# Second-block attention as one software pipeline, with probability blocks turned by 32x32 VectorE transposes and on-chip transfers

## What is computed

```python
x = x + ga * attention(h)            # h = layernorm(x) * (1 + ca) + sa
q = (h @ w_q).reshape(B, S, 8, 4, 128)       # 32 query heads in 8 groups of 4
k = (h @ w_k).reshape(B, S, 8, 128)          # one key head for each group
v = (h @ w_v).reshape(B, S, 8, 128)
scores = einsum('bqhgd,bkhd->bhgqk', q, k) * 128 ** -0.5
scores = where(causal, scores, -inf)
probs  = softmax(scores)
attn   = einsum('bhgqk,bkhd->bqhgd', probs, v).reshape(B, S, 4096)
out    = attn @ w_o
```

## Time and profile before

| | us |
|---|---|
| median of 3 runs | 2140.12 |
| lowest, highest run | 2139.69, 2142.99 |
| span of the profiled execution | 2136.5 |
| PE busy in it | 2033.7 (95%) |
| DVE busy | 1254.4 (59%) |
| ACT busy | 920.2 (43%) |
| POOL busy | 443.5 (21%) |

### The profile page before, as it was taken

One profiled execution on the slowest core, in us unless ns is written; L12 is line 12 of the kernel. 1 busy time (PEld: TensorE's weight loads), 2 busy tenths in 40 slices (PEclk: granted clock), 3 DMA queues, 4 the chain that ended last, 5 costly groups with the idle time before them and its releaser, 6 DMA issues. The chain is left out here.

```text
span 2136.5 us, 33376 instructions
## 1 busy us (share of the span) xinstructions
PE 2033.7 (95%) x10551; PEld 1705.1 (80%) x10551; DVE 1254.4 (59%) x3113; ACT 920.2 (43%) x2453; POOL 443.5 (21%) x446
## 2 busy tenths in 40 slices
PE   6589599999999999999999999999999997999999
PEld 3376388888888888888888888888888885788887
DVE  5854774746556474756756474746647475644444
ACT  3353353535435363543535363543536353623323
POOL 1601732121222122123312122121222211000000
PEclk9679699999999999999999999999999998999999
DMA  9000221000000100001200100000010005410110
GB/s 355 26 1 11 89 69 50 29 20 29 20 29 20 49 29 21 29 0 74 75 30 20 49 14 35 29 20 29 20 49 1 28 10 183 138 60 17 42 59 20
DMA packets 72186, 100.27 MB, mean 47 GB/s; under 512 B 8136, under 2 KB 32712, under 8 KB 72144
## 3 DMA queue, kind: packets, MB, share of 16 engines
q1 hardware_dynamic: 68544, 93.45, 13.0%
q10 hardware_dynamic: 3600, 6.29, 0.8%
HBM read 87.14 MB, written 12.58 MB: 47 GB/s over the span
## 5 line engine op out<-in xcount | busy, mean ns | idle before, releaser
L1121 PE MATMUL ps<-hA,wq 128*128 128x512 f32 x1536 | 384.1, 399 | 0.0
L1195 PE MATMUL ps<-wo,oT 128*128 128x512 f32 x1536 | 368.0, 394 | 0.0
L1279 ACT ACTIVATE probs<-ps,nmax 128x512 f32<-128x512 f32 (+3 forms) x512 | 268.1, 539 | 216.5 <-DVE nmax L1398 216.5
L1195 PEld LDWEIGHTS ps<-wo,oT 128*128 128x128 f32 x1536 | 282.7, 188 | 55.5
L1121 PEld LDWEIGHTS ps<-hA,wq 128*128 128x128 f32 x1536 | 280.3, 188 | 56.1
L1413 DVE TENSOR_TENSOR pt<-ps,pt 128x512 fp32r<-128x512 f32 (+2 forms) x384 | 202.2, 554 | 166.7 <-ACT pt L1289 166.7
L1178 PE MATMUL ps<-pt,V 128*128 128x512 f32 (+2 forms) x1152 | 258.6, 353 | 0.0
L1398 DVE CUSTOM_DVE_ANT_0 ps<-ps,mask 128x512 f32<-128x512 f32 (+3 forms) x512 | 234.6, 519 | 28.3 <-PE ps L1155 28.3
L1155 PE MATMUL ps<-kT,qT 128*128 128x512 f32 (+2 forms) x1152 | 232.7, 346 | 1.1 <-DVE qT L1382 1.1
L1289 ACT ACTIVATE pt<-ps 128x512 fp32r<-128x512 f32 (+2 forms) x384 | 190.5, 496 | 65.8 <-PE ps L1166 64.9
L1155 PEld LDWEIGHTS ps<-kT,qT 128*128 128x128 f32 x1152 | 195.9, 188 | 28.2 <-issue 1.5
(11 more groups left out here) (210 smaller groups left out, 2806.3 us busy)
## 6 DMA issues: line engine op xcount, KB each, us to landing
wq_in<-in_L_attn_w_q_dram SPq DMA_DIRECT2D x17, 1024.0 KB, 7.0
wo_in<-in_L_attn_w_o_dram SPq DMA_DIRECT2D x16, 1024.0 KB, 5.3
wm<-in_L_wmod_dram SPq DMA_DIRECT2D x3, 2048.0 KB, 13.2
wk_in<-in_L_attn_w_k_dram SPq DMA_DIRECT2D x17, 256.0 KB, 2.8
wv_in<-in_L_attn_w_v_dram SPq DMA_DIRECT2D x17, 256.0 KB, 3.3
X<-in_L_attn_x_dram SPq DMA_DIRECT2D x4, 1024.0 KB, 10.6
wm_a<-in_L_wmod_dram SPq DMA_DIRECT2D x2, 2048.0 KB, 22.5
x_mid<-X SPq DMA_DIRECT2D x16, 256.0 KB, 2.0
```

The costliest lines, as they stand in the source:

```text
L1121: last = nc.tensor.matmul(ps[:, bank, :], w[i][:, c, cols], hT[k][:, c, b * S:(b + 1) * S], start=(c == 0 and n == 0), stop=(c == DC - 1 a ...
L1195: last = nc.tensor.matmul(ps[:, bank, :], oT[x_][:, b, h, r * P:(r + 1) * P], wo[y_][:, h, :], start=(h == 0 and n == 0), stop=(h == GQ - ...
L1279: nc.scalar.activation(pe_[:, u % 2, PO[i]:PO[i] + KEYS[i]], ps[:, BANK_S + bank, col:col + KEYS[i]], ACT.Exp, bias=nmax[:, u % 2, i:i + 1 ...
```

## The change

Nothing of the mathematics changes, and no other stage. The changed parts:

- **No PE transposes of probabilities.** POOL, not DVE, multiplies the exponentials by the reciprocal row sum (`body` of POOL, new L1081). DVE turns each 32x32 square in place with five transposes (`turn_quadrants`, new L1454, L1456) into `tp`, which has one buffer. SP then moves the squares across partitions, 16 transfers of 32 partitions x 320 elements (40 KB) for each unit, from `tp` to `pd` (new L992), which has two buffers. ACT makes the high part in one copy of 1280 columns (`p_high`, new L1324), DVE the low part in one subtraction (`p_low`, new L1462). `outputs` reads and writes the four quadrants by a pattern with steps (new L1164).
- **One pipeline.** `scores(u)` runs two units ahead of `outputs(u - 2)`, across the border of two groups. W2 to W7 of a group run in the first five units of the next; K and V of the next group in the last three units of this one. Each pair has an own first body, a loop over the six middle groups, an own last body, and a `flush`.
- **Other moves.** The exponentials have one buffer, not two. The weight loads move from SP's queue to ACT's, ahead of `o_high` in unit 0. Q has one bank, K and V share one, W has two. The gate transposes move from the front to the `flush` of each pair, and so do the load, the normalising and the turning of the next pair's rows. The renamed semaphores (`chosen`, `chain`, `consts`) stand for the same waits.

The diff, cut to its core (the old `turn`, `scale_rows` and `t_part` go):

```diff
+            QD = 32
+            NQD = P // QD
+            SLOTS = 10
+            BW = SLOTS * QD
+            PVS = [(0, 0, 4 * QD), (1, 4 * QD, 7 * QD), (2, 8 * QD, 10 * QD)]
...
-                pe_ = sb(at, "probs", [P, 2, PW], F32)
+                pe_ = sb(at, "probs", [P, PW], F32)
+                tp = sb(at, "tp", [P, NQD, BW], F32)
+                pd = sb(at, "pd", [P, 2, NQD, BW], F32)
+                pt = [sb(at, f"pt{i}", [P, NQD, BW], F32R) for i in range(2)]
...
+                def landed_of(g, u):
+
+                    return landed[u % 2], 256 * (UNITS // 2 * g + (u // 2 + 1))
...
+                            for u in range(UNITS):
+
+                                sp.wait_ge(t_done, UNITS * g + (u + 1))
+                                for a_ in range(NQD):
+                                    for b_ in range(NQD):
+                                        sp.dma_start(pd[QD * b_:QD * (b_ + 1), u % 2, a_, :],
+                                                     tp[QD * a_:QD * (a_ + 1), b_, :]).then_inc(landed[u % 2], 16)
...
+                                pool.wait_ge(rinv_done, UNITS * g + (u + 1))
+                                nc.gpsimd.sem_inc(waits_seen, 1)
+                                for i in range(TB - 1, -1, -1):
+                                    v = pe_[:, PO[i]:PO[i] + KEYS[i]]
+                                    nc.gpsimd.tensor_scalar(v, v, rinv[:, u % 2, i:i + 1], None, ALU.mult).then_inc(scaled, 1)
...
+                        def body(g, first, last):
+                            for u in range(UNITS):
+                                scores(g, u)
+                                if u >= 2 or not first:
+                                    outputs(g, u - 2)
+                                if u == 0:
+                                    turn_v(g, 0)
+                                if u == 4:
+                                    turn_v(g, 1)
+                                if u < 6:
+                                    q_project(g, u + 2)
+                                elif not last:
+                                    q_project(g + 1, u - 6)
+                                if u < 4 and not first:
+                                    out_project(g - 1, u + 2)
+                                if u == 4 and not first:
+                                    out_project(g - 1, 6)
+                                    out_project(g - 1, 7)
+                                if u >= 6:
+                                    out_project(g, u - 6)
+                                if u == 1:
+                                    k_project(g, 1)
+                                if u == 3:
+                                    v_project(g, 1)
+                                if u == 5 and not last:
+                                    k_project(g + 1, 0)
+                                if u == 7 and not last:
+                                    v_project(g + 1, 0)
...
+                        def p_high(g, u):
+                            act.wait_ge(*landed_of(g, u))
+                            reached(act, o_full, UNITS * g + u)
...
+                        def turn_quadrants(g, u):
+
+                            reached(dve, *landed_of(g, u - 1))
+                            to = tp[:].rearrange("p b (s j) -> p s b j", j=QD)
+                            for n, t in enumerate(range(TB - 1, -1, -1)):
+                                dve.wait_ge(scaled, UNITS * TB * g + (TB * u + n + 1))
+                                whole = min(t + 1, TB - 1)
+                                p = pe_[:, PO[t]:PO[t] + KEYS[t]].rearrange("p (s b j) -> p s b j", b=NQD, j=QD)
+                                last = nc.vector.transpose(out=to[:, t:t + 3 * whole - 2:3], in_=p[:, 0:whole])
+                                if t == TB - 1:
+                                    nc.vector.transpose(out=to[:, 7:8], in_=p[:, TB - 1:TB])
+                            last.then_inc(t_done, 1)
```

More of the change, by code:

```diff
@@ new lines, in project, with q_project @@
+                        def project(bank, w, cols, b, done):
+                            for c in range(DC):
+                                for n, (i, k) in enumerate(((0, 0), (0, 1), (1, 0))):
+                                    last = nc.tensor.matmul(ps[:, bank, :], w[i][:, c, cols], hT[k][:, c, b * S:(b + 1) * S],
+                                                            start=(c == 0 and n == 0), stop=(c == DC - 1 and n == 2))
+                            last.then_inc(done, 1)
+                        def q_project(g, u):
+                            h = u % GQ
+                            pe.wait_ge(wq_split, GQ * g + (h + 1))
+                            reached(pe, q_ready, UNITS * g + u)
+                            project(BANK_Q, wq, slice(h * HD, (h + 1) * HD), u // GQ, q_full)
@@ new lines, in outputs @@
+                        def outputs(g, u):
+                            slot, b = u % 2, u % UNITS // GQ
+                            reached(pe, o_ready, UNITS * g + (u + 1))
+                            if u % GQ == 0:
+                                pe.wait_ge(vt_ready, PAIR * g + (b + 1))
+                            pe.wait_ge(plo_done, UNITS * g + (u + 1))
+                            blocks = lambda v: v.rearrange("p a (t j) -> p a t j", j=QD)
+                            by_quadrant = lambda v: v.rearrange("p (t a j) -> p a t j", a=NQD, j=QD)
+                            for n, (kt, first, end) in enumerate(PVS):
+                                for k, (x_, y_) in enumerate(((0, 0), (1, 0), (0, 1))):
+                                    last = nc.tensor.matmul(by_quadrant(ps[:, BANK_O, kt * P:]), V[x_][:, b, kt, :],
+                                                            blocks(pt[y_][:, :, first:end]),
+                                                            start=(n == 0 and k == 0), stop=(n == 2 and k == 2))
+                                if n == 1:
+                                    nc.tensor.matmul(by_quadrant(ps[:, BANK_O, 3 * P:]), v_last[:, b, :],
+                                                     blocks(pd[:, slot, :, LAST]), start=False, stop=False)
+                            last.then_inc(o_full, 1)
@@ new lines, in prologue, with body @@
+                        def prologue(pair, g):
+                            k_high(g, 0)
+                            q_high(g, 0)
+                            v_copy(g, 0)
+                            q_high(g, 1)
+                        def body(g, first, last):
+                            more = not (last and g == NG - 1)
+                            for u in range(UNITS):
+                                if u == 0 and not first:
+                                    v_copy(g, 0)
+                                if u == 2:
+                                    k_high(g, 1)
+                                if u == 4:
+                                    v_copy(g, 1)
+                                if u == 6 and not last:
+                                    k_high(g + 1, 0)
+                                exps(g, u)
+                                if u == 0:
+                                    load_out(g)
+                                    if more:
+                                        load_next(g)
+                                if u >= 2 or not first:
+                                    o_high(g, u - 2)
+                                if u in (0, 4):
+                                    v_high(g, u // 4)
+                                if u >= 1 or not first:
+                                    p_high(g, u - 1)
+                                if u < 6:
+                                    q_high(g, u + 2)
+                                elif not last:
+                                    q_high(g + 1, u - 6)
@@ new lines, in flush @@
+                            if more:
+                                normal(1)
+                            o_low(g, -1)
+                            if more:
+                                parts(0)
+                            add_out(g - 1, 4)
+                            add_out(g - 1, 5)
+                            if more:
+                                parts(1)
+                            add_out(g - 1, 6)
+                            add_out(g - 1, 7)
+                        over_pairs(dve, prologue, body, flush)
```

835 lines of the change are left out of this document (401 added, 434 removed).

## The result

The changed kernel takes **2458.6 us** (median of 4 runs, 2456.75 to 2462.51), the kernel before in the same session 2140.57 (2139.69 to 2142.99). The ratio is 1.149, with a 95% interval of 1.1474 to 1.1506: 318 us slower. The profiled execution has a span of 2457.4 us against 2136.5, which is 320.9 more. The forecast was 2050 us with a range to 2165; the result is on the side of rival 2 and 236 us above the time that rival gave.

A forecast was written before the change was run, and what follows sets the result against it. PE, 95% busy, was taken to bound the kernel. Less work -134, pair ends +46, weight issues +8, between pairs -7, front -2: -89 on 2136.5, plus 3.6 to median: 2051, forecast 2050 us, range 2020 to 2165.

The forecast's parts named there:

- rival 2: SP's chain of sixteen issues and a landing on the one buffer `tp` sets the time: L 12.0, 2223 us; chance 0.19.
- Issues: SP's sixteen transfers of a unit, 0.39 us apart, 5.9 us to the last; bounds 0.33 and 0.50, 5.0 to 7.5 us.
- L: Shortest unit through the transfer loop of `tp`: transposes, issues, landing, hand-overs, 10.0 us against PE's 10.7; bounds 8.0 to 13.3.
- The sign that the text gave for being wrong: DVE waiting for a landing in every unit and PE for `plo_done`, through issues over 0.44 us or transposes over 2.6.
- Transposes: DVE's five instructions over 1280 columns before the transfers of a unit: 1.9 us, bounds 1.3 and 3.2.
- landing: Arrival of a unit's last 40 KB transfer after its issue: 2.0 us, bounds 1.5 and 2.4.
- the ends of the pairs: Rival 1's formula, 46 + 63 L a pair: 20 us to first transposes, 26 after the last; 92 for two.
- Weight loads beside the transfers: ACT's four weight issues delay its `o_high` and high part in unit 0 of each group: 0.5 us a group, +8 us.
- POOL's products: POOL's four scalings by the reciprocal row sum: 1.8 us a unit, 3.3 at worst, hidden under 10.7.
- PE's side: Ten transposes a unit removed, 134 us less work; a group holds 85.9 us; `outputs` runs of 32 elements cost nothing.
- The border between the pairs: PE's 11.5 us gap between the pairs shrinks as loads and normalising move beside W2 to W7: -7 us.
- rival 1: Transfer loop is the bound but a fair one, L from 10.7 to 11.3: 2097 us at 11.0; chance 0.21.

The follow-up runs named there:

- e1: Changed kernel with four of the sixteen transfers of each unit cut in halves, twenty issues for the same bytes: 2770.36 us.
- e2: Changed kernel with four transfers of the same bytes instead of sixteen, leaving out the crossing between bands of partitions (result not the reference's): 2050.41 us.
- e9: Changed kernel with eight of a unit's sixteen transfers issued by SP and eight by ACT, and the products on DVE: 2313.42 us, ratio 1.0795.
- e4: Changed kernel with weight loads cut to one row block of 16 partitions from the second group on, all issues and waits kept: 2398.67 us.
- e3: Changed kernel with the four products by the reciprocal row sum on DVE instead of POOL: 2457.82 us.
- e6: Changed kernel with the squares moved through DRAM, one write and four reads, five issues instead of sixteen: 2102.58 us, ratio 0.981.
- e7: e6 with the products by the reciprocal row sum on DVE instead of POOL: 2078.56 us, ratio 0.970.
- e5: Changed kernel with a second buffer for `tp`, so transposes wait for the landing of two units before: 2275.11 us, ratio 1.0621.
- e10: e5 with the products by the reciprocal row sum on DVE instead of POOL: 2237.43 us, ratio 1.0458.

## Why the prediction was wrong, point by point

- **The step that failed is the term "Issues" of L, and with it the conclusion that the transfer loop hides under PE's 10.7 us.** The term stood as 0.39 us an issue, 5.9 us for fifteen, with 0.50 as the upper bound; measured are 0.63 and 9.4. The price came from two issues in a row at the start of the kernel, of other shapes and other memory. The upper bound was the longest single issue in those rows, and nothing in them excluded more; the lower bound of 0.33 stands in no row that it names. L came out at 13.15 instead of 10.0, and with the break-even at 11.3 that term all but alone brings the +228 of the sum above. L's own bounds, 8.0 to 13.3, just held the measured value, but only by way of slow transposes, and the range of the time stopped at an L of 11.5. The sign that the text gave for being wrong came true: DVE waits for a landing in every unit but two, with issues over 0.44 us. e1 prices the term by adding (0.61), e2 by removing, e9 shows that it belongs to a queue.
- **The other terms of L held.** Transposes 1.75 us (forecast 1.9), landing 1.9 (2.0), and the ends of the pairs were 107 us where 92 stood. Rival 2 had the right mechanism, with 12.0 for L because its price of an issue, 0.50, was too low as well; it had a fifth of the chances.
- **Weight loads beside the transfers** stood as 0.5 us a group, by way of ACT's issues. They cost 5 us a border, 64 in all, by way of the landings; e4 gives back 60. The text had named the 2.5 MB only as an argument for rival 2 and priced them nowhere. The Trainium skill, page DMA: Bandwidth & Descriptors, section Queues, rings and completion order, says that each DMA engine goes round-robin between the queue rows by whole packets; the landings of 6.6 us instead of 1.9 beside 1024 KB loads agree with it, though no run here shows the engines' turns.
- **POOL's products** stood at 1.8 us, at worst 3.3; they take 4.3. The prediction called them hidden at either price. Under a loop of 13.15 us they are, for another reason than the one given (e3: nothing lost). In the short loops they are not (e6 to e7: 24 us, e5 to e10: 38). The price came from a cast of the same width, which is another instruction.
- **PE's side was right.** 134 us less work, 85.9 us a group (e7: 85.9 in the group shown), and `outputs` with its runs of 32 elements costs nothing at full clock: 625.40 to 627.29, 1.89 us, against 1.94 in the earlier trace rows:

```profile
625.40 1.47 PE L1164 MATMUL ps<-pt,V 128*128 128x512 f32 x6
...
627.29 2.90 PE L1110 MATMUL ps<-hA,wq 128*128 128x512 f32 x12
```

- **The border between the pairs** was right in sign: PE's idle stretch of the earlier trace rows is gone altogether, and returns in part as the waits at 1199.81 and 1214.13. No run gives its worth alone.
- **What was missed altogether** is the clock. In a kernel whose PE idles in each unit, work after the idle time runs at the lower level (2.58 us for 1.47, 5.46 for 2.88). In the changed kernel this seems to cost nothing, since the units stay 13.15 us apart beside it, but it makes PE's busy time useless as a measure of its work.
- The Trainium skill's advice on page VectorE: DVE Perf Modes, section Rules for kernel authors, to transpose 128x128 on TensorE, fits the result of the change. The price that rival 1 drew from the 311 ns a block of section The three transpose paths, 3.1 us for ten, did not hold: DVE's part was cheap (269 ns for one 128x128 block of fp32 alone, ten blocks in 1.75 us). What costs is what that section gives as the limit, that only squares of 32x32 are turned: the crossing between bands of partitions is left to do. With the cheaper crossing of e7 the advice does not hold here; that kernel is 3% faster than the one that transposes on TensorE.

## What to carry to other kernels

A loop of many small transfers through one buffer is priced as count x time of one issue on that queue, and that time has to come from a row with the same kind of transfer repeated many times, never from two in a row; where there is none, leave the upper bound open, above all if the forecast turns on it. Fewer and larger transfers win even by a detour: here five issues through DRAM, 640 KB out and in, beat sixteen on-chip ones. They made the change 2% faster than the kernel before instead of 15% slower, and 3% with the products on DVE. The longest wait in a list is not the cause if its releaser waits too. In a loop everyone waits for someone, SP as well; follow the loop once round and look for the part that takes most of the turn.

## What the runs showed of the hardware

- Issues of 32 x 320 fp32 between partitions of SBUF stand 0.63 us apart on SP's queue (sixteen in 10.01) and about 0.67 on ACT's (eight in 5.30, e9). Side by side SP's eight still take 4.97. Reads of 160 KB from DRAM stand about 0.43 apart (four in 1.73, e7).
- 20, 40 and 160 KB on the chip land in 1.8, 1.9 and 3.1 us (e1, e2); the last 40 KB of a lot needed 6.6 beside 2.5 MB of weight loads, and without these bytes (e4) no unit was held up like that.
- POOL's product of fp32 by a scalar per partition takes 1567 ns at 512 columns and 607 at 128, 2.5 ns a column, while its cast of 512 columns takes 610. The Trainium skill, page GPSIMD Engine Reference, section Engine selection, calls one-input work roughly line-rate; the cast agrees with that, the product does not.
- DVE's 32x32 transposes of fp32 over 128 partitions cost 557, 403 and 269 ns for 384, 256 and 128 columns.
